# One round of early scores, another beginning, a spread over two queues, and products nobody reads

## The reference

```python
# layer 0: attention, 32 heads of 8, 8 key/value heads, 1601 keys
q = hidden_state @ Wq + bq
k = encoder_hidden_state @ Wk + bk
v = encoder_hidden_state @ Wv + bv
...
scores = jnp.einsum('bkgld,bksd->bkgls', q, k) * scale
scores = scores + encoder_attention_mask[:, :, None, :, :]
attn = jax.nn.softmax(scores, axis=-1)
out = jnp.einsum('bkgls,bksd->bkgld', attn, v)
...
x = out @ Wo + bo + hidden_state        # then a layer norm
# layer 1: token shift, five mixes, then the recurrence over 256 tokens
def step(s, rkvw):
    r_t, k_t, v_t, w_t = rkvw
    a = k_t[..., :, None] * v_t[..., None, :]
    out = jnp.einsum('bhi,bhij->bhj', r_t, u * a + s)
    s = a + w_t[..., :, None] * s
    return (s, out)
...
x1 = x + og * g @ Wo.T
return x1 + rr * (kk @ Wfv.T)           # kk, rr from a second shift and mix
```

## Time and profile before

| what | value |
|---|---|
| median of 3 runs | 1214.65 us (1214.0 to 1216.17) |
| the profiled execution's own time | 1214.94 us |
| its span, first to last instruction | 1213.1 us |
| PE busy | 1043.7 us, 86% of the span |
| ACT busy | 859.8 us, 71% |
| DVE busy | 631.0 us, 52% |
| POOL busy | 300.4 us, 25% |
| mean granted TensorE clock | 0.948 |

### The profile page before, as it was taken

The page is one execution under the profiler, slowest core; times in us unless marked ns, Lnnn a source line. Parts: engine busy times, 40 slices in busy tenths (PEclk is TensorE's granted clock), DMA queues, the critical chain, the costliest instruction groups (busy, mean ns, idle before and its releaser), DMA issues.

```text
span 1213.1 us, 18191 instructions
## 1 busy us (share of the span) xinstructions
PE 1043.7 (86%) x7100; PEld 376.7 (31%) x7100; DVE 631.0 (52%) x1129; ACT 859.8 (71%) x937; POOL 300.4 (25%) x349
## 2 busy tenths in 40 slices
PE   3059999999999999999999999999998899886664
PEld 1012222332334233333333233323332233323312
DVE  5324032575474656484557546565647344734464
ACT  1127988888878888778888878888787987892010
POOL 6204024041402332231314141224123011400130
PEclk9559999999999999999999999999999999998766
DMA  5643414181317224441427141803352023200310
GB/s 178 164 98 109 111 57 102 19 157 36 85 56 136 34 67 106 64 105 56 109 34 144 57 82 39 161 9 87 87 74 32 2 52 46 35 1 10 50 21 11
DMA packets 65565, 87.47 MB, mean 72 GB/s; under 512 B 8208, under 2 KB 48192, under 8 KB 65472
## 3 DMA queue, kind: packets, MB, share of 16 engines
q1 hardware_dynamic: 63536, 82.91, 31.7%
q0 software_dynamic: 1936, 3.32, 1.0%
HBM read 50.74 MB, written 18.62 MB: 57 GB/s over the span
## 4 chain that ended last, share of the span: by engine, by line
PE 44%; ACT 17%; DVE 14%; issue 12%; DMA 6%; SPq 3%; POOL 2%; POOLq 0%; DVEq 0%; ACTq 0%
PE psum L719 44%; ACT probs L663 15%; DMA vs<-v_c 5%; DVE row_max L1171 3%; DVE vs L1284 2%; DVE vs L1291 2%; SPq L371 2%; POOL vs L557 1%; DVE k_stack L1512 1%; ACT L663 1%; ACT L695 1%; POOL xm L540 1%; DVE xa L1258 1%; SPq L330 1%; POOL vs L548 1%
## 5 line engine op out<-in xcount | busy, mean ns | idle before, releaser
L663 ACT ACTIVATE probs<-psum 128x1024 f32<-128x1024 f32 (+1 forms) x832 | 799.0, 1022 | 219.2 <-PE psum L719 217.6
L719 PE MATMUL psum<-probs,v_aug 128*9 128x512 f32 (+1 forms) x3328 | 415.2, 597 | 0.1
L719 PE MATMUL psum<-q_stack,k_stack 64*128 64x512 bf16 (+1 forms) x1664 | 291.1, 388 | 48.4 <-ACT probs L663 37.0
L719 PEld LDWEIGHTS psum<-q_stack,k_stack 64*128 64x128 bf16 (+1 forms) x1664 | 71.7, 94 | 415.5 <-ACT probs L663 351.5
L557 POOL TENSOR_TENSOR vs<-r_c,vs 128x512 f32<-128x512 f32 x64 | 86.1, 1356 | 103.0 <-DVE tmp L1438 57.5
L719 PEld LDWEIGHTS psum<-probs,v_aug 128*9 128x9 f32 (+1 forms) x3328 | 61.7, 89 | 157.5 <-issue 145.4
L1171 DVE TENSOR_REDUCE row_max<-psum 128x8 f32<-128x1024 f32 x64 | 78.1, 1220 | 45.2 <-PE psum L719 44.7
L1291 DVE TENSOR_TENSOR_SCAN vs<-w_c,vs 128x514 f32<-128x514 f32 x64 | 89.3, 1395 | 21.7 <-POOL vs L548 19.9
L540 POOL TENSOR_TENSOR xm<-tmp,xa 128x512 f32<-128x512 f32 x40 | 43.0, 1090 | 207.8 <-DVE tmp L1278 207.8
L1218 DVE COPY o_raw<-psum 128x512 f32<-128x512 f32 x32 | 22.1, 690 | 96.8 <-PE psum L719 96.7
L719 PE MATMUL psum<-k_stack,q_stack 48*128 48x128 bf16 x512 | 26.5, 223 | 46.1 <-DMA q_stack<-q_stacked 29.8
(11 more groups left out here) (175 smaller groups left out, 1072.1 us busy)
## 6 DMA issues: line engine op xcount, KB each, us to landing
vs<-v_c SPq DMA_DIRECT2D x64, 257.0 KB, 7.6
ctx_t<-in_mask SPq DMA_DIRECT2D x8, 1601.0 KB, 6.5
k_stacked<-k_parts SPq DMA_DIRECT2D x48, 200.1 KB
k_stack<-k_stacked SPq DMA_DIRECT2D x32, 300.2 KB, 6.7
ctx_t<-in_ctx_t SPq DMA_DIRECT2D x24, 400.0 KB, 6.4
q_stacked<-q_parts SPq DMA_DIRECT2D x96, 64.0 KB, 2.5
q_stack<-q_stacked SPq DMA_DIRECT2D x32, 192.0 KB, 7.2
ctx_t<-in_ctx_t SPq DMA_DIRECT2D x8, 401.0 KB, 6.3
```

Of the source, the lines that this page charges most:

```text
L663: nc.scalar.activation(probs[turn_step % NP][t][0:w, :, :], ps[t][0:w, :, :], ACT.Exp).then_inc(exped.sem, 1)
L719: return nc.tensor.matmul(dst, lhsT, rhs, start=start, stop=stop)
```

## The change

Five things are changed together.

1. **One round.** The shift is taken from the first 32 keys instead of 128. All 32 products of a half of the heads fit into the two banks, so four rounds become one (`A_ROUND = 33`, `B_ROUND = 10`), followed by two reductions of 512 numbers each. DVE's order is changed to match, and the turn of the shift moves from step 14 to 12.
2. **The beginning.** The context of sample 0 is loaded before the query weights; DVE clears one half of the stacks and POOL the other; PE projects into four banks without waiting for ACT, and multiplies its zeros afterwards; ACT loads its table of functions early; the keys are split in two halves of 801 and 800 columns, alternating on ACT and DVE; half of the query stores and half of the first stack loads are issued by ACT's queue; sample 1's context is loaded right after sample 0's projection, and the mask of sample 0 is loaded and reduced only in iteration 7 (`mask_turn`). The order of the late loads is changed, and they start after POOL's clearing.
3. **The spread.** For the last sample, five of the eight spreads are issued by SP and three by POOL; POOL makes the last mix before its second piece of the state, not after it.
4. **The flag.** `count_over` moves behind the fourth mix of iteration 8, `raise_flag` to just before the second residual of that iteration, PE's product for it from step 8 to 26.
5. **Products nobody reads.** In the iteration without attention (`b is None and c is not None`) PE makes `FILLERS[step]` products of 64 x 128 by 64 x 512 in bf16 into bank 0 ahead of the side work of that step, 81 in all.

```diff
-KV_FIRST = (7, 5, 7, 5)
+KV_FIRST = (0, 1, 2, 3)
-A_ROUNDS = [31, 32, 33, 34]
-B_ROUNDS = [9, 10, 11, 12]
+A_ROUND, B_ROUND = 33, 10
+
+FILLERS = {10: 24, 12: 7, 16: 6, 36: 2, 38: 3, 44: 20, 48: 11, 50: 8}
+LAST_SPREAD = ((0, 2, 4, 6, 7), (1, 3, 5))
+FIRST_KEYS = 32
...
+        def mask_turn(a):
+            return (a - 1) % B
...
@@ SP, all_turns @@
                 if not general:
-                    load_mask(lo)
+                    sp.dma_start(w_q[:, :, :], ...).then_inc(early_q.sem, 16)
+                    sp.dma_start(chan[:, :, :], dram["chan"]).then_inc(early_q.sem, 16)
+                    sp.dma_start(ident[:, :], dram["ident"]).then_inc(early_q.sem, 16)
+                sp.wait_ge(kv_proj.sem, kv_proj.at(lo))
+                load_ctx(lo + 1)
+                sp.wait_ge(q_proj.sem, q_proj.at(lo))
+                load_x_t(lo + 1)
+                if not general:
                     sp.wait_ge(cleared.sem, 1)
+                    sp.wait_ge(cleared_up.sem, 1)
                 store_k_parts(lo)
-                store_q_parts(lo)
-                load_stacks(lo, 0)
+                store_q_parts(lo, (1,))
+                load_stacks(lo, 0, (0,))
...
+                        if step == 2 and it == hi - 1 and not general:
+                            load_mask(lo)
...
-                            spread_v(c)
+                            spread_v(c, range(HD) if it < hi else LAST_SPREAD[0])
@@ POOL @@
+            def spread_rest(c):
+                pool.wait_ge(v_ready.sem, v_ready.at(c))
+                pool.wait_ge(gathered.sem, gathered.at(c - 1))
+                for j in LAST_SPREAD[1]:
+                    spread_digit(pool, j, spread_last[j])
...
                             mixed(c, n)
+                            if n == 1 and b is None:
+                                spread_rest(c)
                         first_state(c, 0)
+                        mixed(c, 4)
                         first_state(c, 1)
-                        mixed(c, 4)
...
+            link(nc.gpsimd.memset(k_stack[1][32:64, :, :], 1.0))
+            link(nc.gpsimd.memset(q_stack[1][32:64, :, :, :], 0.0))
+            link(nc.gpsimd.memset(k_stack[1][96:128, :, :], 1.0))
+            nc.gpsimd.memset(q_stack[1][96:128, :, :, :], 0.0).then_inc(cleared_up.sem, 1)
@@ ACT, project @@
+                biased(0)
+                biased(1)
+                high(0)
+                biased(2)
+                mid(0)
+                biased(3)
+                high(1)
+                mid(1)
...
+                act.wait_ge(q_low.sem, q_low.at(a))
+                store_queries(act, a, 0)
+                act.wait_ge(cleared.sem, 1)
+                act.wait_ge(k_out.sem, k_out.at(a))
+                act.wait_ge(q_out.sem, q_out.at(a))
+                load_stack_half(act, a, 0, 1)
@@ PE @@
+            def sub_round(n, g):
                 pe.wait_ge(stack_in[g].sem, stack_in[g].at(n))
-                pe.wait_ge(sub_reduced[g].sem, sub_reduced[g].at(n, r))
-                for u in range(4):
+                for u in range(16):
+                    t, pair, hd, lc = u // 8, u // 4 % 2, u // LC % 2, u % LC
                     for half in range(2):
                         p0 = HALF * half
-                        last = mm(psum[:, 6 + half, P * u:P * u + P],
+                        last = mm(psum[:, 6 + half, FIRST_KEYS * u:FIRST_KEYS * u + FIRST_KEYS],
...
-                                  k_stack[g][p0:p0 + DOT, t, 0:P])
+                                  k_stack[g][p0:p0 + DOT, t, 0:FIRST_KEYS])
...
+            def keep_going(n):
+                for _ in range(n):
+                    mm(bank(0), k_stack[0][0:HALF, 0, 0:P], q_stack[0][0:HALF, 0, 0:2, :])
...
+                if b is None and c is not None:
+                    keep_going(FILLERS.get(step, 0))
...
-                    if n >= 2:
-                        pe.wait_ge(kv_biased.sem, kv_biased.at(a, n - 1))
                     project_kv(a, n, KV_FIRST[n])
+                pe.wait_ge(early_q.sem, early_q.at(0))
                 project_q(a, 6)
...
-                        if it == B and step == 8 and not general:
+                        if it == B and step == 26 and not general:
@@ DVE @@
+            def reduce_round(n, g):
+                dve.wait_ge(sub_scored[g].sem, sub_scored[g].at(n))
+                for half in range(2):
+                    last = nc.vector.tensor_reduce(row_max[...][:, :, half, :],
+                                                   bank(6 + half)..., AX.X, ALU.max)
+                last.then_inc(sub_reduced[g].sem, 1)
...
+                    if it == lo + B - 1 and not general:
+                        see_mask(lo, 0)
+                        see_mask(lo, 1)
...
-                    if it == B and not general:
-                        count_over()
-                        raise_flag()
...
                     if b is not None:
-                        reduce_step(b, 1, 0, general)
-                        reduce_step(b, 1, 1, general)
+                        reduce_step(b, 1, general)
+                        negate_shift(b, 1)
...
+                        if it == B and not general:
+                            dve.wait_ge(xt_turned.sem, xt_turned.at(c))
+                            count_over()
...
-                    if a is not None:
-                        reduce_step(a, 0, 2, general)
-                        reduce_step(a, 0, 3, general)
+                        reduce_step(a, 0, general)
                         negate_shift(a, 0)
```

More of the change, by code:

```diff
@@ L35 @@
 HALF_STEPS = STEPS // GQ
+SPLIT = [(0, 801), (801, 800)]
 NP = 3
@@ L223, in build @@
         stack_in = [sig(f"stack_in{g}", 64) for g in range(GQ)]
[L224 to L225 removed]
+        sub_scored = [sig(f"sub_scored{g}") for g in range(GQ)]
+        sub_reduced = [sig(f"sub_reduced{g}") for g in range(GQ)]
         shift_neg = [sig(f"shift_neg{g}") for g in range(GQ)]
@@ L273, in late_loads @@
             c = dram
-            yield heads[:, :], c["heads"]
-            for m in range(HD):
-                yield heads_turned[16 * m:16 * m + 16, :], c["ident"][0:16, 0:16]
             yield w_o[:, :, :], c["L0_xattn_Wo"].rearrange("(c p) n -> p c n", p=P)
@@ L280, in late_loads @@
             yield w1[:, :, :], c["L1_xattn_maa_w1"].rearrange("(c p) n -> p c n", p=P)
+            for n in ["Wr", "Wk", "Wfk", "Wfr", "Wfv"]:
+                yield wsq[n][:, :, :], c[n + "_t"].rearrange("(c p) n -> p c n", p=P)
+            yield raw_v[:, :, :], c["Wv_t"].rearrange("(c p) n -> p c n", p=P)
+            yield raw_g[:, :, :], c["Wg_t"].rearrange("(c p) n -> p c n", p=P)
+            yield heads[:, :], c["heads"]
+            for m in range(HD):
+                yield heads_turned[16 * m:16 * m + 16, :], c["ident"][0:16, 0:16]
             for f in range(4):
@@ L337, in load_stacks @@
                 sp.wait_ge(q_out.sem, q_out.at(n))
-                for half in range(2):
-                    k0, p0 = 4 * g + 2 * half, HALF * half
-                    sp.dma_start(k_stack[g][p0:p0 + DOT, :, :],
-                                 k_st_d[n % B][k0:k0 + 2].rearrange("k r d s -> (r d) k s")).then_inc(stack_in[g].sem, 16)
-                    sp.dma_start(q_stack[g][p0:p0 + DOT, :, :, :].rearrange("p t h l -> p (t h) l"),
-                                 q_st_d[n % B][4 * k0:4 * k0 + 8].rearrange("h r d l -> (r d) h l"))\
-                      .then_inc(stack_in[g].sem, 16)
+                for half in halves:
+                    load_stack_half(sp, n, g, half)
             def shift_to_dram(n, g):
@@ L642, in project, with biased @@
             def project(a):
+                turn = a // B
                 act.wait_ge(early_in.sem, early_in.at(0))
-                for n, (at, w) in enumerate(PIECE):
+                def biased(n):
+                    at, w = PIECE[n]
                     act.wait_ge(kv_proj.sem, kv_proj.at(a, n + 1))
@@ L990, in side @@
                 if b is not None:
-                    if step == 14:
+                    if step == 12:
                         turn_shift(b, 1)
@@ L1075, in first_projection @@
                 else:
-                    for r in range(4):
-                        sub_round(a, 0, r)
+                    sub_round(a, 0)
                 turn_shift(a, 0)
@@ L1339, in all_turns @@
                 keep_v(lo, 1, 7)
-                if not general:
-                    see_mask(lo, 0)
-                    see_mask(lo, 1)
-                for r in range(4):
-                    reduce_step(lo, 0, r, general)
+                reduce_step(lo, 0, general)
                 negate_shift(lo, 0)
@@ L1496, in all_turns @@
                     if c is not None:
+                        if it == B and not general:
+                            raise_flag()
                         dve.wait_ge(x1_done.sem, x1_done.at(c))
```

208 lines of the change are left out of this document (110 added, 98 removed).

## The result

The changed kernel takes 1176.98 us (median of 4 runs, 1173.51 to 1179.08), the kernel before, on the same chip, 1215.41 (1214.0 to 1217.5). The ratio is 0.968, with a 95% interval of 0.9648 to 0.9711. 38.4 us are saved where 58.3 were forecast: faster, as said, but 6 us outside the range. The profiled execution took 1178.83 us with a span of 1176.9.

What follows compares the result with a forecast made beforehand. Bounds: a chain of transfers and small operations first, PE's order of work in the middle, one sample's chain through all engines last. Savings 28 + 12 + 4 + 2.5 - 0.2 + 12 = 58.3 gave 1156.5 us, range 1144 to 1171.

Steps and rivals of the forecast that it cites:

- I add 2 and take 49: Beginning: first scores at 47, plus 2 us for crowded transfers, so 49 instead of 77.27, saving 28 us.
- first scores at 56: Rival for the beginning: late weights crowd the stores and stack loads; time 1164 us, chance 0.17.
- the lower bound, 21: Beginning: least saving allowed, with DMAs near saturation all along, 7 us later than the 28 us case.
- The clock, "8.9" and "1.4": Iteration 8: fillers keep PE's clock warm, saving 8.9 us on the path and 1.4 in the last sum and means.
- don't hold the clock, or run cold and delay: Rival for the tail: fillers in half the rows fail, only the flag's 1.7 us stays; 1168 us, chance 0.08.
- The flag, 1.7: Iteration 8: moving the count and the flag off the path before the scaled input saves 1.7 us.
- The rounds of `a` and `b`, 12 and 4: Middle: one round instead of four saves 12 us at `a` (iterations 1 to 6), 4 at `b` (1 to 7).
- X: Middle: PE's time for the new round of 32 products, 0.3 to 1.05 us, taken as 0.65.
- Iteration 0, 2.5: Iteration 0: reductions queue behind two mask reductions, so one round saves about 2.5 us (1 to 4).
- the mask, -0.2: Iteration 7: sample 0's mask adds 3.6 us of DVE work, costing 0.2 us (0 to 3.6).
- the spread, 0: Iteration 8: issuing the last sample's spread on two queues saves 0 us (0 to 0.5).
- rare combinations: Cases left outside the range 1144 to 1171 us, besides the slower case of the raised flag (about 2270, chance 0.02).

Runs made afterwards that it cites:

- h1: Changed kernel with the late weights issued by GpSimd behind its split of sample 1's queries and keys in iteration 0; 1170.91 us.
- g1: Changed kernel with late weights issued once sample 0's shift has landed, and sample 0's mask reductions moved from iteration 7 to 8; 1172.38 us.
- h4: Changed kernel with the edits of h1, h2 and h3 together; 1154.67 us, ratio 0.9501 to the kernel before.
- h2: Changed kernel with fillers in pairs over both halves of the rows, as many as fit each PE wait of iteration 8; 1168.12 us.
- e1: Changed kernel without any of the products nobody reads; 1178.46 us.
- h3: Changed kernel with ten more fillers over 128 rows in PE's wait ahead of step 42 in iterations 6 and 7; 1174.39 us.
- f2: Changed kernel with fillers over all 128 rows instead of 64, same number, type and columns; 1171.61 us.
- f3: Changed kernel with each filler doubled into a pair, one in the upper and one in the lower 64 rows; 1169.9 us.
- f1: Changed kernel with f32 fillers of 128 rows and 256 columns, in nearly the same time by forecast; 1172.03 us.

## Why the prediction was wrong

It was right on the direction, on the bound of each regime and on most of the working, and failed in two terms, both of which it had named as rivals.

- **Contention, "I add 2 and take 49".** This step failed. The crowd cost 7.6 to 7.9 us (56.12 against 48.52 in h1 and 48.24 in g1), and 8.6 to 9.7 if counted from the first key store (38.3 us from there in the changed kernel, 29.7, 29.6 and 28.6 in h1, g1 and h4); without it the first scores come at the forecast 49 or before. The sum priced the issue and "a landing" by an engine at 0.45: the six stores took 8.75 instead of 4.3, and the wait for the last of them 8.2 instead of 1.5. The rival "first scores at 56" is what happened, to 0.1 us, and the 21.15 saved are the lower bound, 21. The two shares of the earlier trace rows, 0.61 and 0.45, add up to 1.06: the rows themselves suggested that the engines would be full, and sample 1's context, 1.6 MB more, came on top. The argument against it, that most of the late loads are small, counted loads, not bytes. The Trainium skill ("DMA: Bandwidth & Descriptors", Issuing engines are not separate DMA queues) says that a second issuing engine saves only the sequencer's time. The trace agrees where the engines were full: six stores on SyncE took as long as twelve. Where they weren't, in h1 at a DMA share of 0.64, six took 5.11.
- **The clock, "8.9" and "1.4".** This step failed. The way in which I priced a warm clock was right: in h2, where the clock holds, the tail is 13.5 us shorter than before, more than the forecast 12, though with more fillers than the prediction had. That these fillers hold it was assumed. They used 64 of 128 rows. They kept a clock that was warm already for 10 us (1077 to 1087; without them, in e1, it fell at about 1081), lost it behind a wait of 1.20, and from 1132 on ran at 0.50 for 32 us. The rival "don't hold the clock, or run cold and delay", which I gave 0.08, was what happened; its 1168 was too low mainly because the contention came too (h1, with the same fillers and without the contention, took 1170.91). With both, 49 becomes 56, and of 12 nothing is left: 1156.5 + 7 + 12.5 = 1176. The middle's missing 2.7 bring that to 1178.7, where the profiled execution was (1178.83); the median of the four lies 1.85 under it.
- **The flag, 1.7.** Right where it was taken: in e1 xn's turn stands 12.23 us behind the last Wo of attention instead of 13.98, 1.75 sooner. (The copy of `v_c` stands at 27.85 instead of 30.37, but there the clock has a part: the product ahead, `h_a`, took 1.13 instead of 2.08.) It was given back at once, since Wk then ran cold.
- **The rounds of `a` and `b`, 12 and 4.** Nearly right. Iterations 1 to 5 gained 2.5 to 2.65 each, as forecast; X was 0.49 where I took 0.65. Iteration 6 gained 1.1 and iteration 7 lost 0.7. With the falls of the clock gone (h3) they gain 2.35 and 0.6. So 2.5 us went to two falls that the kernel before didn't have, nearly all of the 2.7 that the middle missed.
- **Iteration 0, 2.5; the mask, -0.2; the spread, 0.** 2.15 was measured for the first. The mask costs nothing (g1). From `v_c` to the sum `o_c` both kernels take 36.4 and 36.5 us, so no gain of issuing the spread on two queues shows.
- **The range.** It left out "rare combinations", and a combination came. Two rivals of 0.17 and 0.08 with different causes should have been added up once before the range was closed.

What stays open is when the clock falls in iterations 5 to 7 behind waits of 2.8 us and less. h3 showed that filling the wait of iterations 6 and 7 prevents it there; what decides in which of the others it falls wasn't found. Nor was it found why f2 and f3 lost the clock under Wk and f1, with the same wait of 1.09 ahead of it, didn't. Fillers over 64 rows in every wait were not run, so how much of h2's gain over f3 (3.7 us of tail) they would have had is open. In f2, f3, g1 and h2 the stretch before the tail was about 3 us longer, most of it by such falls, in parts of the code that were not changed (in g1 2.8 more were GpSimd's). Four runs of the changed kernel spread over 5.6 us.

## What to carry to other kernels

Before transfers are moved earlier, add the shares of the stretches that will fall together: here they came to 1.06, and the chain of small stores and loads that everything waits for paid, in its issue and more in its landing. Where that threatens, the bulk load belongs behind that whole chain, and behind what its issuing engine owes to others. Fillers for the clock should use all 128 rows, or two halves side by side, and stand in every wait of the stretch. Against the tail of the kernel before (105.7), fillers over 64 rows gave -0.6 to 2.9 us here, over 128 rows 7.2 to 9.9, and over 128 rows in every wait 13.5. Price two likely mishaps together, too.

## What the hardware showed that I had not expected

- PE was busy for 31.2 of 32 us, about 19 of them with fillers over 64 rows, at a clock of 0.50. With the fillers over 128 rows the clock stayed at 1.00 for 23 us at the other place where the single ones had lost it (1079 to 1102 in f2), and with pairs in every wait for 82 us.
- Two products in the two halves of the rows take 0.22 us together, as long as one (24 pairs in 5.36, 24 single ones in 5.35).
- An f32 product that the code calls once stands twice in the trace (21 calls as 42 products, 0.22 us each), one in bf16 once (24 as 24).
- The same wait of 2.84 us was followed by 3.3 us at half clock in one kernel and by none in another, at the same place of the code.
- A DVE operation of 0.36 us on 128 x 32 numbers took 2.56 us and ended 0.04 us after the GpSimd subtraction beside it; in the changed kernel one of 0.28 took 2.38 (90.43 to 92.81) beside GpSimd's of 89.66 to 92.68. The Trainium skill ("SBUF — State Buffer", Terms) says that DVE and GpSimd share a port pair, held for a whole instruction; both rows agree.
- A query store of 64 KB landed 2.0 us after its issue before (median) and 9.2 us in the changed kernel, with a DMA share of 1.07 while they were issued.
- With the transfer engines full, a store of the shift and its way back, 24 KB (32 x 3 x 128 in bf16), took 10.1 us instead of 4.8.
